# One set of sums instead of two: VectorE adds three tiles of probabilities into the buffer in which POOL adds the other five

## The chip, the core and the metric

The kernel runs on one core of a Trainium2 chip. The engines of the core work side by side and meet at semaphores: TensorE (PE in the profile; its weight loads are listed as PEld), VectorE (DVE), ScalarE (ACT), GpSimd (POOL) and SyncE (SP), which issues the DMAs. The metric is the device time of one execution in microseconds (us).

## The reference

A transformer block on x of 4 batches x 1024 tokens x 128 columns, all float32:

```
x = x + attention(layernorm(x))
x = x + ffn(layernorm(x))

attention: qkv = xn @ w_qkv; 16 heads of 64; q and k rotated (RoPE)
           scores = q k^T / 8;  probs = softmax(scores)     # over 1024 keys
           out = (probs @ v) @ w_out + b_out
ffn:       fp4_linear(silu(fp4_linear(x, w_gate)) * fp4_linear(x, w_up), w_down)
           # activations and weights rounded to FP4 in blocks of 16, then multiplied
```

The change concerns one quantity of the softmax: for each query and head, the sum of the exponentials over the 1024 keys.

## The kernel before

Attention takes most of the kernel. Its unit is a **pair**: two heads of one batch, so 4 x 8 = 32 pairs, P = 0 to 31. The 1024 queries of a pair are cut into two **halves** c = 0, 1 of 512, its keys into eight tiles jt = 0 to 7 of 128. One **exp step** i = 8c + jt (16 in a pair) is: eight score matmuls into PSUM `st` (keys on partitions, 512 queries, both heads), one exponential on ScalarE from `st` into one of eight slots of the ring `probs`, and the products with `v` into PSUM `po`. The scores carry the row maximum as a fourth product with `max_rows`, so that the exponential needs no further subtraction. Row maxima come from separate score matmuls, one pair ahead: TensorE fills `mx` (L1099), VectorE reduces it to `negmax` (L800). There is a single `mx`, so a fill waits until the reduction of the fill before is done (semaphore `mx_free`), 16 times in a pair.

All engines walk over the same two loops, written out by hand: over pairs, and in a pair over d = 0 to 7. On TensorE a d is: a fill of `mx`, the scores of two exp steps, a second fill of `mx`, one small unit of preparation or finishing through the PSUM bank `ms`, the products with v of the two steps before, and perhaps a second unit. The units are given by a table: K (d = 0 to 3, projection of keys and queries of pair P+2, then rotated on VectorE at L832 and L833), V (d = 4, 5), O (d = 6, 7, output projection of pair P-1, added on VectorE at L847), B (the maxima are transposed, L1106, and VectorE spreads them into `max_rows`, L814; at d = 2 for the second half of P, at d = 6 for the first half of P+1), and S (the softmax sums, L1115; at d = 5 for the first half of P, at d = 1 for the second half of P-1). In a few pairs X and Y units transpose the next batch's and the finished batch's rows.

The sum over keys of one half is made in three places. VectorE adds tiles 0 and 1 (`first_keys`, L822) into `first_sum`, one instruction for each of the two heads, at d = 1 and 3 for the first half and at d = 5 and 6 for the second. POOL adds tiles 2 and 3 into `psum_keys` and then tiles 4 to 7 to it, one at a time (`add_step`, L352), five instructions for each half; on POOL's queue they stand among the rotations (L483), the low parts of the heads (L487), the normalisation of the output (L478) and, in the pairs P = 13, 14, 21, 22, 29 and 30, three instructions that round FP4 values (`round_y`, L367 to L369), which stand between the add of tile 3 and that of tile 4. TensorE then sums over the partitions by products with ones (`softmax_sums`, L1115), four for `first_sum` and four for `psum_keys`, in one accumulation group. An exponential may overwrite a slot of the ring only when the product with v and the adder of that tile are done (L595 to L598).

The semaphore `key_part` counts VectorE's instructions, `key_sum` POOL's. After the last pair a second stage (the FFN) follows on the same engines, whose start on TensorE stands behind the last S unit.

Of the kernel before, what the change touches and what calls it, by code (L numbers as in the profile page):

```python
# [11 lines left out]
ALU = mybir.AluOpType  # L12
# [21 lines left out]
FIRST_KEYS = 2  # L34
# [22 lines left out]
def block_program(nc, ctx, x_d, gamma_d, beta_d, wqkv_d, wout_d, bout_d, wg_d, wu_d, wd_d,  # L57
# [34 lines left out]
    first_sum = sb("first_sum", [PART, 2, 2, CH])  # L92
# [35 lines left out]
    h_exp = [t[:, :].rearrange("p c a n -> p (c a n)")[:, 0:GT * FFN] for t in (psum_keys, first_sum)]  # L128
# [78 lines left out]
    def keys_added(P, c):  # L207

        return (JT - FIRST_KEYS - 1) * (2 * P + c)
# [119 lines left out]
    def _(pool):  # L329
# [10 lines left out]
        def add_step(P, i):  # L340
            c, jt = i // JT, i % JT
            if jt <= FIRST_KEYS:
                return
            wait(pool, exp_done, STEPS * P + i + 1)
            if jt == FIRST_KEYS + 1:
                if P > 0:
                    filled(pool, ("S", P - 1, c))
                first = probs[:, (STEPS * P + i - 1) % RING]
            else:
                pool.wait_ge(key_sum, keys_added(P, c) + jt - FIRST_KEYS - 1)  # L350
                first = psum_keys[:, c]
            nc.gpsimd.tensor_tensor(psum_keys[:, c], first, probs[:, (STEPS * P + i) % RING], ALU.add)\  # L352
              .then_inc(key_sum, 1)
# [187 lines left out]
    def _(act):  # L541
# [47 lines left out]
        def exp(P, i):  # L589
            step_n = STEPS * P + i  # L590
            act.wait_ge(st_ps, step_n + 1)
            if step_n >= RING:
# [4 lines left out]
                else:  # L597
                    act.wait_ge(key_sum, keys_added(old, c) + max(jt - FIRST_KEYS, 1))  # L598
# [92 lines left out]
    def _(dve):  # L691
# [126 lines left out]
        def first_keys(P, c, a):  # L818
# [3 lines left out]
            nc.vector.tensor_reduce(first_sum[:, c, a], probs[:, 0:FIRST_KEYS, a].rearrange("p r n -> p n r"), AX.X,  # L822
# [26 lines left out]
        def pair(P):  # L849
            F = P - 1  # L850
            for d in range(JT):
# [6 lines left out]
                for kind, X, u in units_at(P, d):  # L858
                    if kind == "K":
                        rope_parts(X, u)  # L860
                    if kind == "B":
                        spread_maxima(X, u)
                    if kind == "O" and present(P):
                        accumulate(X, u)
                if present(P) and d in (1, 3, 5, 6):
                    first_keys(P, d // HALF, int(d in (3, 6)))
# [136 lines left out]
    def _(pe):  # L1003
# [104 lines left out]
        def softmax_sums(F, c):  # L1108
            bank(("S", F, c))
            pe.wait_ge(key_part, 2 * (2 * F + c) + 2)  # L1110
            pe.wait_ge(key_sum, keys_added(F, c + 1))
            for part in (first_sum, psum_keys):
                for j in range(4):
                    a, quarter = j // 2, bass.ts(j % 2, QUARTER)
                    last = mm(ms[32 * j:32 * j + 32, 0:QUARTER], ones[:, 0:32], part[:, c, a, quarter],  # L1115
                              start=part is first_sum, stop=part is psum_keys)
# [153 lines left out]
```

## Time and profile before

| | |
|---|---|
| median of 3 runs | 1718.77 us (1718.58 to 1719.2) |
| profiled execution | 1719.78 us, its span 1718.0 us |
| granted TensorE clock, mean | 0.979 of full |
| PE busy | 93% of the span |
| POOL busy | 75% |
| DVE busy | 69% |
| ACT busy | 42% |

The profile is of one execution. Busy time is the time in which an engine had an instruction in work; matmuls are pipelined, so that two rows of TensorE overlap a little, and the distance between starts says more than a duration. A wait in brackets at the end of a row of a timeline is idle time of the engine just before the row, with what ended it.

### The profile page before, as it was taken

How to read it: one execution, taken by the hardware profiler on the slowest of the kernel's cores; microseconds unless marked ns; L12 is line 12 of the kernel's file. 1: busy time of each engine (PE TensorE's matmuls, PEld its weight loads, DVE VectorE, ACT ScalarE, POOL GpSimd, SP SyncE). 2: the span in 40 equal slices, each digit the busy share in tenths (PEclk: the TensorE clock that was granted, in tenths of full speed). 3: DMA queues.
4: the chain of work that ended last, by engine and by line, in shares of the span. 5: the costliest groups of instructions: out<-in, count | busy, mean ns of one | idle time of the engine just before them, and what ended most of it. 6: DMA issues, size and time to landing. Idle time of an engine off the chain costs nothing.

```text
span 1718.0 us, 26114 instructions
## 1 busy us (share of the span) xinstructions
PE 1605.0 (93%) x10025; PEld 863.4 (50%) x10025; DVE 1180.9 (69%) x1440; ACT 722.2 (42%) x941; POOL 1294.3 (75%) x729
## 2 busy tenths in 40 slices
PE   3899999999999999999999999999999999997666
PEld 1455555555555555555545555555555545554454
DVE  4877776666667677766667767766667777654676
ACT  1244444544444544544444445444444534443222
POOL 4478888777778878887777878797777788865674
PEclk9799999999999999999999999999999999998888
DMA  4111111111111111111111111111111111100000
GB/s 123 42 38 33 44 44 43 38 45 44 40 35 35 44 33 44 44 36 44 45 44 40 26 44 36 40 44 39 42 45 44 40 36 34 27 16 21 13 13 25
DMA packets 69194, 67.12 MB, mean 39 GB/s; under 512 B 26512, under 2 KB 52432, under 8 KB 69072
## 3 DMA queue, kind: packets, MB, share of 16 engines
q1 hardware_dynamic: 69072, 65.46, 15.2%
q8 instruction: 80, 1.31, 0.3%
q14 instruction: 42, 0.34, 0.1%
HBM read 29.25 MB, written 2.62 MB: 19 GB/s over the span
## 4 chain that ended last, share of the span: by engine, by line
PE 83%; DVE 13%; POOL 1%; issue 1%; ACT 1%; DMA 0%; DVEq 0%; POOLq 0%
PE po L1059 27%; PE st L1047 24%; PE mx L1099 9%; PE ms L1082 8%; PE ms L1070 4%; PE ms L1115 4%; PE ms L1124 4%; DVE negmax L800 3%; DVE first_sum L822 2%; DVE max_rows L814 1%; PE ms L1106 1%; PE mx L1183 1%; DVE probs L756 1%; PE st L1183 1%; DVE amax L750 1%
## 5 line engine op out<-in xcount | busy, mean ns | idle before, releaser
L800 DVE TENSOR_REDUCE negmax<-mx 128x2 f32<-128x1024 f32 x504 | 615.6, 1221 | 376.4 <-PE mx L1099 376.4
L599 ACT ACTIVATE probs<-st 128x1024 f32<-128x1024 f32 x512 | 497.8, 1023 | 533.6 <-PE st L1047 533.6
L352 POOL TENSOR_TENSOR psum_keys<-psum_keys,probs 128x1024 f32<-128x1024 f32 x256 | 607.4, 2373 | 127.4 <-ACT probs L599 109.3
L1059 PE MATMUL po<-probs,v 128*64 128x512 f32 x2048 | 495.7, 605 | 0.0
L1047 PE MATMUL st<-heads 64*128 64x512 f32 x3072 | 440.0, 391 | 0.0
L1047 PEld LDWEIGHTS st<-heads 64*128 64x128 f32 x3072 | 289.9, 185 | 58.4 <-issue 2.4
L1099 PE MATMUL mx<-heads 64*128 64x512 f32 x1008 | 230.1, 452 | 29.7 <-DVE negmax L800 29.5
L1059 PEld LDWEIGHTS po<-probs,v 128*64 128x64 f32 x2048 | 124.2, 136 | 256.2 <-issue 147.0
L352 POOL TENSOR_TENSOR psum_keys<-probs 128x1024 f32<-128x1024 f32 x64 | 151.7, 2370 | 87.1 <-ACT probs L599 87.0
L1047 PE MATMUL st<-max_rows,one_rows 64*128 64x512 f32 x1024 | 201.9, 389 | 0.0
L1099 PEld LDWEIGHTS mx<-heads 64*128 64x128 f32 x1008 | 94.8, 184 | 186.3 <-issue 117.3
L483 POOL TENSOR_TENSOR kq<-kq 128x1024 f32<-128x1024 f32 x64 | 152.3, 2379 | 40.8 <-DMA kq<-sin_part 40.7
L1082 PE MATMUL ms<-xnT,wqkv 128*128 128x512 f32 x256 | 150.9, 673 | 15.4 <-DVE sin_part L833 13.5
L822 DVE TENSOR_REDUCE first_sum<-probs 128x512 f32<-128x1024 f32 x128 | 159.4, 1245 | 5.1 <-ACT probs L599 5.1
L487 POOL TENSOR_TENSOR heads<-kq,heads 128x1024 fp32r<-128x1024 f32 x64 | 153.6, 2401 | 0.0
L478 POOL TENSOR_TENSOR oT<-oT,rsum 128x512 f32<-128x512 f32 x64 | 82.8, 1293 | 84.7 <-DMA rsum<-recips 83.2
L1047 PEld LDWEIGHTS st<-max_rows,one_rows 64*128 64x128 f32 x1024 | 96.9, 185 | 21.8
L832 DVE TENSOR_TENSOR kq<-ms,cos 128x512 f32<-128x512 f32 x128 | 87.4, 683 | 17.7 <-issue 9.0
L814 DVE TENSOR_TENSOR max_rows<-ms,mask 128x512 fp32r<-128x512 f32 x64 | 44.3, 691 | 70.7 <-PE ms L1106 70.7
L611 ACT ACTIVATE sums_kept<-ms 128x256 f32<-128x256 f32 x64 | 24.6, 385 | 151.4 <-PE ms L1115 151.4
L833 DVE TENSOR_TENSOR sin_part<-ms,sin 128x512 f32<-128x512 f32 x128 | 87.0, 680 | 0.0
L617 ACT ACTIVATE oT<-po 128x512 f32<-128x512 f32 x64 | 38.3, 599 | 109.8 <-PE po L1059 109.8
(144 smaller groups left out, 1237.0 us busy)
## 6 DMA issues: line engine op xcount, KB each, us to landing
kq<-sin_part SPq DMA_DIRECT2D x256, 128.0 KB, 2.4
rsum<-recips SPq DMA_DIRECT2D x128, 128.0 KB, 2.9
wqkv<-in_L_attn_w_qkv_dram SPq DMA_DIRECT2D x32, 192.0 KB, 2.8
resid<-in_L_attn_x_dram SPq DMA_DIRECT2D x4, 512.0 KB, 8.3
wout<-in_L_attn_w_out_dram SPq DMA_DIRECT2D x32, 64.0 KB, 2.6
out_dram<-resid SPq DMA_DIRECT2D x8, 256.0 KB, 2.3
sums<-sums_kept SPq DMA_DIRECT2D x64, 4.0 KB
spread<-sums SPq DMA_DIRECT2D x64, 4.0 KB, 1.5
```

Source lines behind the costliest of these rows:

```text
L352: nc.gpsimd.tensor_tensor(psum_keys[:, c], first, probs[:, (STEPS * P + i) % RING], ALU.add)\
L483: nc.gpsimd.tensor_tensor(raw[s], raw[s], swp[s], ALU.add).then_inc(rotated, 1)
L487: nc.gpsimd.tensor_tensor(heads[:, L % SETS, s, 1], raw[s], heads[:, L % SETS, s, 0].bitcast(F32), ALU.subtract)\
L599: nc.scalar.activation(probs[:, step_n % RING], st[step_n % 2][:, :], ACT.Exp, scale=SCALE)\
L800: nc.vector.tensor_reduce(negmax[:, t // HALF, :, t % HALF, half], banks[:, :], AX.X, ALU.max, negate=True)\
L822: nc.vector.tensor_reduce(first_sum[:, c, a], probs[:, 0:FIRST_KEYS, a].rearrange("p r n -> p n r"), AX.X, ALU.add).then_inc(key_part, 1)
L832: nc.vector.tensor_tensor(raw[s][:, part], ms[:, :], cos[:, part], ALU.mult).then_inc(cos_done, 1)
L833: nc.vector.tensor_tensor(sin_part[:, s, part], ms[:, :], sin[:, part], ALU.mult).then_inc(ms_free, 1)
L1047: last = mm(st[step_n % 2][:, a], stationary[rows], moving[rows], start=(n == 0), stop=(n == 3))
L1059: last = mm(po[HD * a:HD * a + HD, :], v[:, P % 2, jt, HD * a:HD * a + HD], probs[:, step_n % RING, a], start=(jt == 0), stop=(jt == JT - 1))
L1082: mm(ms[:, :], wqkv[:, L % 2, 1 - s, :], batch(L)[:, bass.ts(c, CH)], start=True, stop=True)\
L1099: last = mm(banks[:, a, :], heads[rows, N % SETS, 1, 0, bass.ts(t, PART)], heads[rows, N % SETS, 0, 0, bass.ts(half, CH)], start=True, sto ...
```

## The change

VectorE now adds three tiles, 0 to 2, and writes the sum into `psum_keys` itself. POOL adds the five tiles 3 to 7 to that, still five instructions for each half; the first of them now waits for both of VectorE's instructions of that half. TensorE multiplies one buffer with ones, four products for each half and not eight. VectorE's four instructions of a pair stand at d = 1, 2, 5 and 6 (before: 1, 3, 5 and 6), and at d = 2 and 6 in front of `spread_maxima`, where before `spread_maxima` stood in front of the one at d = 6. The old buffer stays as a work buffer of the FFN.

```diff
-FIRST_KEYS = 2
+FIRST_KEYS = 3
...
     def keys_added(P, c):
-        return (JT - FIRST_KEYS - 1) * (2 * P + c)
+        return (JT - FIRST_KEYS) * (2 * P + c)
...
         def add_step(P, i):
             c, jt = i // JT, i % JT
-            if jt <= FIRST_KEYS:
+            if jt < FIRST_KEYS:
                 return
             wait(pool, exp_done, STEPS * P + i + 1)
-            if jt == FIRST_KEYS + 1:
-                if P > 0:
-                    filled(pool, ("S", P - 1, c))
-                first = probs[:, (STEPS * P + i - 1) % RING]
-            else:
-                pool.wait_ge(key_sum, keys_added(P, c) + jt - FIRST_KEYS - 1)
-                first = psum_keys[:, c]
-            nc.gpsimd.tensor_tensor(psum_keys[:, c], first, probs[:, (STEPS * P + i) % RING], ALU.add)\
+            if jt == FIRST_KEYS:
+                pool.wait_ge(key_part, 2 * (2 * P + c) + 2)
+            wait(pool, key_sum, keys_added(P, c) + jt - FIRST_KEYS)
+            nc.gpsimd.tensor_tensor(psum_keys[:, c], psum_keys[:, c], probs[:, (STEPS * P + i) % RING], ALU.add)\
               .then_inc(key_sum, 1)
...
-                    act.wait_ge(key_sum, keys_added(old, c) + max(jt - FIRST_KEYS, 1))
+                    act.wait_ge(key_sum, keys_added(old, c) + jt - FIRST_KEYS + 1)
...
-            nc.vector.tensor_reduce(first_sum[:, c, a], probs[:, 0:FIRST_KEYS, a].rearrange("p r n -> p n r"), AX.X,
+            nc.vector.tensor_reduce(psum_keys[:, c, a], probs[:, 0:FIRST_KEYS, a].rearrange("p r n -> p n r"), AX.X,
                                     ALU.add).then_inc(key_part, 1)
...
                 for kind, X, u in units_at(P, d):
                     if kind == "K":
                         rope_parts(X, u)
+                    if kind == "O" and present(P):
+                        accumulate(X, u)
+                if present(P) and d in (1, 2, 5, 6):
+                    first_keys(P, d // HALF, int(d in (2, 6)))
+                for kind, X, u in units_at(P, d):
                     if kind == "B":
                         spread_maxima(X, u)
-                    if kind == "O" and present(P):
-                        accumulate(X, u)
-                if present(P) and d in (1, 3, 5, 6):
-                    first_keys(P, d // HALF, int(d in (3, 6)))
...
         def softmax_sums(F, c):
             bank(("S", F, c))
-            pe.wait_ge(key_part, 2 * (2 * F + c) + 2)
             pe.wait_ge(key_sum, keys_added(F, c + 1))
-            for part in (first_sum, psum_keys):
-                for j in range(4):
-                    a, quarter = j // 2, bass.ts(j % 2, QUARTER)
-                    last = mm(ms[32 * j:32 * j + 32, 0:QUARTER], ones[:, 0:32], part[:, c, a, quarter],
-                              start=part is first_sum, stop=part is psum_keys)
+            for j in range(4):
+                a, quarter = j // 2, bass.ts(j % 2, QUARTER)
+                last = mm(ms[32 * j:32 * j + 32, 0:QUARTER], ones[:, 0:32], psum_keys[:, c, a, quarter],
+                          start=True, stop=True)
             last.then_inc(ms_full, 1)
```

On VectorE at d = 2, between the two reductions of `mx`, the order before was this (L832 and L833 are the rotation, L814 the spreading of the maxima):

```order
L800 TENSOR_REDUCE negmax<-mx 128x2 [waits mx_full] x2
L832 TENSOR_TENSOR kq<-ms,cos 128x512 [waits swap_q_in,lo_done,ms_full]
L833 TENSOR_TENSOR sin_part<-ms,sin 128x512
L814 TENSOR_TENSOR max_rows<-ms,mask 128x512 [waits st_ps,ms_full]
L800 TENSOR_REDUCE negmax<-mx 128x2 [waits mx_full] x2
```

The same place after (four lines are gone above, so L796, L828, L829, L818 and L810 are the old L800, L832, L833, L822 and L814):

```order
L796 TENSOR_REDUCE negmax<-mx 128x2 [waits mx_full] x2
L828 TENSOR_TENSOR kq<-ms,cos 128x512 [waits swap_q_in,lo_done,ms_full]
L829 TENSOR_TENSOR sin_part<-ms,sin 128x512
L818 TENSOR_REDUCE psum_keys<-probs 128x512 [waits exp_done]
L810 TENSOR_TENSOR max_rows<-ms,mask 128x512 [waits st_ps,ms_full]
L796 TENSOR_REDUCE negmax<-mx 128x2 [waits mx_full] x2
```

A sum of keys has come in, in front of the spreading.

On VectorE at d = 6 it was (L847 adds the output projection):

```order
L800 TENSOR_REDUCE negmax<-mx 128x2 [waits mx_full] x2
L847 TENSOR_TENSOR resid<-ms,resid 128x512 [waits ms_free,ms_full]
L814 TENSOR_TENSOR max_rows<-ms,mask 128x512 [waits st_ps,ms_full]
L822 TENSOR_REDUCE first_sum<-probs 128x512 [waits exp_done]
L800 TENSOR_REDUCE negmax<-mx 128x2 [waits mx_full] x2
```

And after:

```order
L796 TENSOR_REDUCE negmax<-mx 128x2 [waits mx_full] x2
L843 TENSOR_TENSOR resid<-ms,resid 128x512 [waits ms_free,ms_full]
L818 TENSOR_REDUCE psum_keys<-probs 128x512 [waits exp_done]
L810 TENSOR_TENSOR max_rows<-ms,mask 128x512 [waits st_ps,ms_full]
L796 TENSOR_REDUCE negmax<-mx 128x2 [waits mx_full] x2
```

The sum of keys and the spreading have changed places.

On POOL the adds of a pair's first half were, with the rotation L483 among them:

```order
L352 TENSOR_TENSOR psum_keys<-probs 128x1024 [waits ms_full,exp_done]
L352 TENSOR_TENSOR psum_keys<-psum_keys,probs 128x1024 [waits key_sum,exp_done] x3
L483 TENSOR_TENSOR kq<-kq 128x1024 [waits swap_k_in,cos_done]
L352 TENSOR_TENSOR psum_keys<-psum_keys,probs 128x1024 [waits key_sum,exp_done]
L478 TENSOR_TENSOR oT<-oT,rsum 128x512 [waits po_copied,recips_in]
```

And are now:

```order
L348 TENSOR_TENSOR psum_keys<-psum_keys,probs 128x1024 [waits key_sum,key_part,exp_done]
L348 TENSOR_TENSOR psum_keys<-psum_keys,probs 128x1024 [waits key_sum,exp_done] x3
L479 TENSOR_TENSOR kq<-kq 128x1024 [waits swap_k_in,cos_done]
L348 TENSOR_TENSOR psum_keys<-psum_keys,probs 128x1024 [waits key_sum,exp_done]
L474 TENSOR_TENSOR oT<-oT,rsum 128x512 [waits po_copied,recips_in]
```

Nothing has moved in the queue; the first add waits for `key_part`.

## Rows read from the trace of the kernel before

**Rows 1.** The page, busy time by engine: us (share of the span) xinstructions.

```profile
PE 1605.0 (93%) x10025; PEld 863.4 (50%) x10025; DVE 1180.9 (69%) x1440; ACT 722.2 (42%) x941; POOL 1294.3 (75%) x729
```

**Rows 2.** Waits over the whole span: total us, times, longest.

```profile
PE mx L1099 <- DVE negmax L800: 29.5, 35, 3.5
```

**Rows 3.** Timeline of PE, P = 14, d = 1 to 5, and d = 1 after: start, us, ...

```profile
735.92 0.64 PE L1115 MATMUL ms<-first_sum,ones 128*32 128x256 f32 x8
736.38 0.61 PE L1115 MATMUL ms<-psum_keys,ones 128*32 128x256 f32 x8
736.92 0.50 PE L1099 MATMUL mx<-heads 64*128 64x512 f32 x2
...
739.09 0.40 PE L1099 MATMUL mx<-heads 64*128 64x512 f32 x2
739.42 1.13 PE L1082 MATMUL ms<-xnT,wqkv 128*128 128x512 f32 x2
...
744.79 0.39 PE L1099 MATMUL mx<-heads 64*128 64x512 f32 x2
...
758.98 0.64 PE L1115 MATMUL ms<-first_sum,ones 128*32 128x256 f32 x8
...
783.66 0.64 PE L1115 MATMUL ms<-first_sum,ones 128*32 128x256 f32 x8
```

**Rows 4.** Timeline of DVE, P = 14, d = 1 and 2.

```profile
735.69 1.24 DVE L822 TENSOR_REDUCE first_sum<-probs 128x512 f32<-128x1024 f32 x1
737.47 1.23 DVE L800 TENSOR_REDUCE negmax<-mx 128x2 f32<-128x1024 f32 x1 [0.54 <-PE mx L1099]
...
741.27 0.68 DVE L833 TENSOR_TENSOR sin_part<-ms,sin 128x512 f32<-128x512 f32 x1
742.71 0.69 DVE L814 TENSOR_TENSOR max_rows<-ms,mask 128x512 fp32r<-128x512 f32 x1 [0.75 <-PE ms L1106]
```

**Rows 5.** Timeline of DVE, P = 14, d = 6.

```profile
763.74 0.68 DVE L847 TENSOR_TENSOR resid<-ms,resid 128x512 f32<-128x512 f32 x1
765.81 0.69 DVE L814 TENSOR_TENSOR max_rows<-ms,mask 128x512 fp32r<-128x512 f32 x1 [1.39 <-PE ms L1106]
766.42 1.26 DVE L822 TENSOR_REDUCE first_sum<-probs 128x512 f32<-128x1024 f32 x1
767.60 1.22 DVE L800 TENSOR_REDUCE negmax<-mx 128x2 f32<-128x1024 f32 x1
```

**Rows 6.** Timeline of PE, P = 14, d = 7.

```profile
765.70 0.50 PE L1099 MATMUL mx<-heads 64*128 64x512 f32 x2
...
768.86 0.50 PE L1099 MATMUL mx<-heads 64*128 64x512 f32 x2 [0.80 <-DVE negmax L800]
769.29 1.16 PE L1124 MATMUL ms<-wout,oT 128*128 128x128 f32 x8
```

**Rows 7.** Groups by line and shape, DVE: busy us, mean ns.

```profile
L750 DVE TENSOR_REDUCE amax<-probs 128x88 f32<-128x1408 f32 x8 | 12.9, 1614 | 0.1
```

**Rows 8.** Timeline of DVE, P = 1, d = 1.

```profile
120.57 0.86 DVE L712 BATCH_NORM_STATS2 ln_columns<-resid 128x6 f32<-128x128 f32 x4
```

**Rows 9.** Timeline of POOL, P = 14, d = 1 to 4.

```profile
736.30 1.29 POOL L367 TENSOR_TENSOR xnT<-xnT,y_exp 128x512 f32<-128x512 f32 x1
...
740.06 4.91 POOL L352 TENSOR_TENSOR psum_keys<-psum_keys,probs 128x1024 f32<-128x1024 f32 x2
...
747.49 2.38 POOL L483 TENSOR_TENSOR kq<-kq 128x1024 f32<-128x1024 f32 x1
749.82 2.37 POOL L352 TENSOR_TENSOR psum_keys<-psum_keys,probs 128x1024 f32<-128x1024 f32 x1
```

**Rows 10.** Timeline of DVE, last pair, d = 6.

```profile
1558.19 1.23 DVE L822 TENSOR_REDUCE first_sum<-probs 128x512 f32<-128x1024 f32 x1
```

**Rows 11.** Timeline of POOL, last pair, tiles 4 to 7 of the second half.

```profile
1556.69 9.90 POOL L352 TENSOR_TENSOR psum_keys<-psum_keys,probs 128x1024 f32<-128x1024 f32 x4 [1.64 <-ACT probs L599]
```

**Rows 12.** Timeline of PE, last S unit.

```profile
1566.74 0.64 PE L1115 MATMUL ms<-first_sum,ones 128*32 128x256 f32 x8 [0.61 <-POOL psum_keys L352]
```

More of the change, by code:

```diff
@@ L91, in block_program @@
     probs = sb("probs", [PART, RING, 2, CH])
-    first_sum = sb("first_sum", [PART, 2, 2, CH])
+    tail_work = sb("tail_work", [PART, 2, 2, CH])
     psum_keys = sb("psum_keys", [PART, 2, 2, CH])
@@ L127, in block_program @@
     hT = probs_flat[:, 4 * GT * FFN:4 * GT * FFN + GT * 3 * PART]
-    h_exp = [t[:, :].rearrange("p c a n -> p (c a n)")[:, 0:GT * FFN] for t in (psum_keys, first_sum)]
+    h_exp = [t[:, :].rearrange("p c a n -> p (c a n)")[:, 0:GT * FFN] for t in (psum_keys, tail_work)]
     st = [ctx.enter_context(nc.psum_tensor(f"st{i}", [PART, 2, CH], F32)) for i in range(2)]
```

## The prediction

> **What bounds the kernel now.** I read the page's busy shares first: PE is busy 93% of the span [rows 1], so what TensorE does not issue is time won, and what it waits for is time lost. Second, the list of waits: in attention TensorE waits for little else than VectorE's reductions of `mx`, 35 times, 29.5 us [rows 2]. Third, the timelines of PE, DVE and POOL over one pair, P = 14, since the list doesn't say at which d. The reader is to see there that in each pair TensorE is held once: the second fill of `mx` at d = 7 starts 3.16 us after the first [rows 6], where at d = 2 it is 2.17 [rows 3]. I counted 31 such waits of 0.79 to 0.82 us, one in each pair but the last. Their cause is VectorE at d = 6: it idles 1.39 us for the transposed maxima, spreads them, and only then sums keys, so that the reduction of `mx` comes late [rows 5]. POOL has slack; its adds set no time before the last pair, where the last S unit waits 0.61 us for them [rows 12].
>
> **The products with ones.** An S unit is two groups, the second 0.46 us behind the first, the next fill of `mx` 0.54 behind the second [rows 3]. One group goes. If the one that stays keeps the longer distance, 0.46 is won, otherwise up to 0.54. I take 0.46, for 64 units: **-29.4** (to -34.6).
>
> **The price of a third tile on VectorE.** It appears in no row. A reduction of 1408 elements takes 1.61 us [rows 7], one of 1024 takes 1.23 with two outputs and 1.24 to 1.26 with 512 [rows 4, 5]: it goes by what is read, 1.0 ns an element. 1536 elements give 1.24 + 0.53 = 1.77. The next instruction starts 0.08 before a row's end (766.42 + 1.26 against 767.60), so the sum holds the queue 1.69 to 1.70 us, where it held 1.16 to 1.18. From below the bound is 1.24 (price by outputs), from above 1.5 x 1.245 = 1.87 (nothing fixed); the row with 1408 is nearest, I take 1.77.
>
> The Trainium skill (VectorE: DVE Perf Modes, "The TRN2 errata") gives 58 cycles and one per element at 0.96 GHz for an instruction that reads SBUF, 1.66 us for 1536 elements. By the same formula 1024 elements would take 1.13, and the row shows 1.24, so the row decides. With 1.66 the sum below would be some 10 us better, 1698.
>
> **VectorE at d = 1 and 2.** How a late reduction hurts is in rows 6: it ends at 768.82, the fill starts 0.04 later, and the next unit 0.43 after the fill, where it is 0.33 otherwise [rows 3]. So a wait costs its lateness plus 0.10. At d = 1 the sum starts at 735.69 as now, the next reduction at 737.39 instead of 737.47 [rows 4], but TensorE comes 0.46 earlier. The reduction ends at 738.61, the second fill is possible at 738.65 and due at 739.09 - 0.46 = 738.63 [rows 3]: 0.12 lost, 30 pairs, **+3.6**. In P = 0 and 1 four statistics stand behind the sum, 0.78 on the queue [rows 8]: **+1.6**.
> At d = 2 a whole sum is new. In the clock of the trace before, the last product of the rotation frees the queue at 741.87, the sum runs to 743.57, covering the 0.75 of idle time [rows 4]; spreading 0.61, reduction 1.22, fill at 745.44, due at 744.79 [rows 3]: 0.65 + 0.10 = 0.75 for each of the 30 pairs with K units, and 0.6 in P = 30: **+23.1**. That it left d = 3 gives nothing: there VectorE was in time. After d = 3 it has caught up.
>
> **VectorE at d = 6.** The sum now starts behind the addition, 763.74 + 0.61 = 764.35, and lies in the idle 1.39 us [rows 5]. It ends at 766.05, spreading at 766.66, reduction 767.88, fill 767.92, due at 765.70 + 2.17 = 767.87. Lost 0.05 + 0.10 = 0.15 instead of 0.99 + 0.10 = 1.09 [rows 6]: 0.94 won in 31 pairs, **-29.1**.
>
> **POOL.** Its first add waited for an exponential of d = 1 and now waits for the sum at d = 2, about 743.65 + 0.12 + 0.1 = 743.9, some 9 us later; behind it in the queue stand the other adds, the rotations, the low parts and the normalisation. Four adds of 2.5 (4.91 for two, one 2.37 [rows 9]), rotation 2.33, add 2.37: tile 7 done at 758.6. The S unit of d = 5 is due at 758.98 + 0.12 + 0.75 = 759.85 [rows 3]: 1.3 us of cover, no cost. The second half in the same way: VectorE's sum 766.6 (0.12 + 0.75 - 0.46 later than above), an add and a low part 4.7, four adds 9.9, done 781.2, due at 783.66 + 0.41 - 0.94 = 783.1 [rows 3]; this pair has a Y unit of 0.6, the others 1.3 us of cover. Who waits for what stands behind the adds (the rotated and low parts, the ring slots) wants it later than the S units want the sum.
> The cover is gone in two places. Where `round_y` stands between the adds, POOL needs 3.76 more [rows 9] and is at 762.2: 2.35 us of waiting in five pairs, 1.1 in P = 30: **+12.9**; the scaling of `y` in three pairs costs about **+0.3**. And in the last pair nothing is left behind which POOL could hide: VectorE's sum waits there for the addition of d = 6 and starts at 1558.19 [rows 10]. POOL's first add of that half, which ran before 1556.69 [rows 11], starts at 1558.19 + 1.77 + 0.1 = 1560.1, five take 12.4, S at 1572.6 instead of 1566.74 [rows 12], and the FFN behind it, where VectorE is the first to have work: **+5.9**.
>
> **Sum.** -29.4 - 29.1 + 3.6 + 1.6 + 23.1 + 12.9 + 0.3 + 5.9 = -11.1. From the profiled 1719.78 that is 1708.7; the median of the runs shown lies 1.0 below that execution, so 1707.7.
>
> **Rivals.**
> - *The third tile costs half of the first two* (1.87 us). Each 0.1 us more on this sum costs at d = 1, 2 and 6, about 91 times: +9, so 1717. For it: no row has this shape with three. Against: 1408 elements in 1.61.
> - *The third tile is free*, 1.24 us, as far as 512 outputs set the price. d = 1 costs nothing, d = 2 0.22 for 30 pairs, d = 6 wins its whole 1.09: 1681. Against it stand rows 7.
> - *POOL is late at every S unit* (slower). The place is the start of tile 3's add; cover is 1.3 us, and 57 S units have only that. If the hand-over from VectorE and the five adds take 1.7 us more than worked out, 57 x 0.5 + 6 x 1.7 = 39 are added: 1746. It decides from 1.5 us on. For it: a chain of 15 us on POOL now starts at a fixed point with no idle time in it. Against: all adds take 2.37 us or 2.5 behind one another, whatever VectorE does beside them [rows 9, 11].
> - *The rounding and the last pair cost less than worked out*, because something in these pairs moves with POOL: without the 12.9, 1695.
>
> **How the numbers follow.** The forecast has 0.72, the costly third tile 0.10, the free one 0.04, POOL late at every S unit 0.08, no cost in the rounding pairs 0.06. The range of 8 in 10 goes from 1695 (longer saving on the products, no cost in the rounding pairs) to 1719 (the costly tile with the small waits doubled). About 0.2% (3.4 us) is what a measurement can tell from no change: faster than 1715.3 holds for most of the forecast, the free tile and the last rival, 0.79; the costly tile and a small part of the forecast fall within, 0.12; slower 0.09.
>
> **What would show it.** In the changed profile: L1111 with 4 x 64 products of weights, 8 matmul rows an S unit and the next fill 0.54 behind its start; L818 at 1.77 us; the wait of 0.80 at d = 7 gone, and one of about 0.5 idle at d = 3 in its place; POOL's first add released by DVE; S units that wait over 2 us for POOL only near the six rounding pairs; the last S unit held some 6 us. A sum of keys at 1.9 or more, or a wait for POOL at ordinary S units, would make the forecast wrong.

## The result, and the profile after

| | before | changed |
|---|---|---|
| median | 1719.39 us (10 runs, 1716.95 to 1720.7) | 1722.95 us (10 runs, 1721.7 to 1725.57) |
| span of the profiled execution | 1718.0 us | 1720.2 us |
| ratio to before, 95% interval | | 1.0023 (1.0013 to 1.0032) |

The change made the kernel slower by 3.6 us, where 11 us less was forecast: wrong sign, and outside the range. The forecast of 1707.7 is out by 15 us.

Busy time by engine on the page of the changed kernel, as in [rows 1]:

```profile
PE 1589.5 (92%) x9513; PEld 846.0 (49%) x9513; DVE 1256.0 (73%) x1440; ACT 722.8 (42%) x941; POOL 1293.1 (75%) x729
```

TensorE has its 512 fewer matmul rows. VectorE is busy 75 us more in all. Its 128 sums alone take 244.4 us; at the 1.24 to 1.26 of [rows 4, 5] they took 160, so each is 0.66 longer, where I had 0.53 (the sums grew by 85 us; 10 are taken back by more overlap of rows and by slightly shorter other rows). The group of these sums on the page (busy us, mean ns, idle before):

```profile
L818 DVE TENSOR_REDUCE psum_keys<-probs 128x512 f32<-128x1536 f32 x128 | 244.4, 1910 | 9.2 <-ACT probs L595 9.2
```

**1.91 us, not 1.77**, and more than the upper bound of 1.87. This row is where the forecast failed. The waits of TensorE in the changed kernel (total, times, longest), to be read beside [rows 2]:

```profile
PE mx L1096 <- DVE negmax L796: 23.3, 33, 3.5
PE ms L1110 <- POOL psum_keys L348: 18.1, 11, 6.6
```

The first total is hardly lower than before, but the waits are other ones. The timeline of PE in P = 14, d = 1 to d = 7, answers to [rows 3, 6]:

```profile
729.98 0.64 PE L1110 MATMUL ms<-psum_keys,ones 128*32 128x256 f32 x8
730.55 0.49 PE L1096 MATMUL mx<-heads 64*128 64x512 f32 x2
...
732.84 0.50 PE L1096 MATMUL mx<-heads 64*128 64x512 f32 x2
...
739.41 0.49 PE L1096 MATMUL mx<-heads 64*128 64x512 f32 x2 [0.61 <-DVE negmax L796]
...
755.99 1.08 PE L1110 MATMUL ms<-psum_keys,ones 128*32 128x256 f32 x8 [2.26 <-POOL psum_keys L348]
757.00 0.79 PE L1096 MATMUL mx<-heads 64*128 64x512 f32 x2
...
763.83 0.51 PE L1096 MATMUL mx<-heads 64*128 64x512 f32 x2
...
766.16 0.49 PE L1096 MATMUL mx<-heads 64*128 64x512 f32 x2
```

The S unit takes 0.57 us to the next fill instead of 1.00. At d = 7 the two fills are 2.33 apart, no longer 3.16: the old wait is gone. In its place the second fill of d = 3 (739.41) waits 0.61, and in this rounding pair the S unit waits 2.26 for POOL. The timeline of DVE at d = 2 and at d = 6 shows the cause, beside [rows 4, 5]:

```profile
735.72 1.91 DVE L818 TENSOR_REDUCE psum_keys<-probs 128x512 f32<-128x1536 f32 x1
737.54 0.69 DVE L810 TENSOR_TENSOR max_rows<-ms,mask 128x512 fp32r<-128x512 f32 x1
738.14 1.22 DVE L796 TENSOR_REDUCE negmax<-mx 128x2 f32<-128x1024 f32 x1
...
762.47 1.90 DVE L818 TENSOR_REDUCE psum_keys<-probs 128x512 f32<-128x1536 f32 x1
764.29 0.68 DVE L810 TENSOR_TENSOR max_rows<-ms,mask 128x512 fp32r<-128x512 f32 x1
764.89 1.21 DVE L796 TENSOR_REDUCE negmax<-mx 128x2 f32<-128x1024 f32 x1
```

A sum holds the queue 1.82 us, from its start to that of the spreading.

**An ordinary pair, by four marks.** The transposition B and the S unit each stand once in each half of a pair, so their starts cut it into four pieces. Before, PE:

```profile
860.29 0.33 PE L1106 MATMUL ms<-ident,maxcol 128*128 128x128 f32 x1
877.92 0.64 PE L1115 MATMUL ms<-first_sum,ones 128*32 128x256 f32 x8
...
884.34 0.33 PE L1106 MATMUL ms<-ident,maxcol 128*128 128x128 f32 x1
900.93 0.64 PE L1115 MATMUL ms<-first_sum,ones 128*32 128x256 f32 x8
...
907.41 0.33 PE L1106 MATMUL ms<-ident,maxcol 128*128 128x128 f32 x1
```

The same pair in the changed kernel:

```profile
857.24 0.33 PE L1103 MATMUL ms<-ident,maxcol 128*128 128x128 f32 x1
874.06 0.64 PE L1110 MATMUL ms<-psum_keys,ones 128*32 128x256 f32 x8
880.28 0.33 PE L1103 MATMUL ms<-ident,maxcol 128*128 128x128 f32 x1
897.76 0.64 PE L1110 MATMUL ms<-psum_keys,ones 128*32 128x256 f32 x8
903.78 0.33 PE L1103 MATMUL ms<-ident,maxcol 128*128 128x128 f32 x1
```

The pieces went from 17.63, 6.42, 16.59 and 6.48 us to 16.82, 6.22, 17.48 and 6.02. The first holds the wait of d = 7 (-0.81, -0.84 in most pairs), the second an S unit and the new lateness at d = 2 (-0.20), the third the wait of d = 3 (+0.89), the fourth an S unit alone (-0.46, -0.44 in most). A pair is 0.58 shorter; the forecast was 0.99 (0.92 and 0.94 won, 0.12 and 0.75 lost).

### The profile page after: what moved, and what is told of

Its sections match the earlier page's. It is cut to its first block, busy times and chain, and to the rows that moved or that the text cites. A ratio compares the mean times of both kernels' runs of the same rounds, so it can differ in the third digit from the quotient of the medians.

```text
span 1720.2 us, 25092 instructions
## 1 busy us (share of the span) xinstructions
PE 1589.5 (92%) x9513; PEld 846.0 (49%) x9513; DVE 1256.0 (73%) x1440; ACT 722.8 (42%) x941; POOL 1293.1 (75%) x729
## 4 chain that ended last, share of the span: by engine, by line
PE 65%; DVE 14%; POOL 11%; issue 7%; ACT 1%; DMA 1%; SPq 1%; POOLq 0%; DVEq 0%; ACTq 0%
PE st L1044 21%; PE po L1056 19%; PE mx L1096 8%; POOL psum_keys L348 8%; PE ms L1079 5%; PE ms L1119 3%; PE ms L1067 3%; DVE psum_keys L818 3%; DVE negmax L796 3%; PE ms L1110 2%; DVE kq L828 1%; DVE sin_part L829 1%; PE mx L1178 1%; DVE max_rows L810 1%; DVE probs L752 1%
## 5 line engine op out<-in xcount | busy, mean ns | idle before, releaser
L348 POOL TENSOR_TENSOR psum_keys<-psum_keys,probs 128x1024 f32<-128x1024 f32 x320 | 762.3, 2382 | 311.4 <-issue 241.6
L796 DVE TENSOR_REDUCE negmax<-mx 128x2 f32<-128x1024 f32 x504 | 616.6, 1223 | 366.9 <-PE mx L1096 366.9
L595 ACT ACTIVATE probs<-st 128x1024 f32<-128x1024 f32 x512 | 497.8, 1024 | 536.1 <-PE st L1044 536.1
L1096 PE MATMUL mx<-heads 64*128 64x512 f32 x1008 | 235.9, 464 | 23.3 <-DVE negmax L796 23.3
L818 DVE TENSOR_REDUCE psum_keys<-probs 128x512 f32<-128x1536 f32 x128 | 244.4, 1910 | 9.2 <-ACT probs L595 9.2
L483 POOL TENSOR_TENSOR heads<-kq,heads 128x1024 fp32r<-128x1024 f32 x64 | 151.6, 2369 | 0.0
L828 DVE TENSOR_TENSOR kq<-ms,cos 128x512 f32<-128x512 f32 x128 | 87.5, 683 | 17.7 <-issue 9.0
L829 DVE TENSOR_TENSOR sin_part<-ms,sin 128x512 f32<-128x512 f32 x128 | 87.0, 680 | 0.0
L618 ACT ACTIVATE heads<-kq 128x1024 fp32r<-128x1024 f32 x64 | 67.3, 1052 | 28.9 <-POOL kq L479 28.9
L1067 PE MATMUL ms<-wqkv,xnT 128*128 128x128 f32 x512 | 74.1, 288 | 1.7 <-DVE sin_part L829 1.7
```

The source lines that it names most:

```text
L348: nc.gpsimd.tensor_tensor(psum_keys[:, c], psum_keys[:, c], probs[:, (STEPS * P + i) % RING], ALU.add)\
L483: nc.gpsimd.tensor_tensor(heads[:, L % SETS, s, 1], raw[s], heads[:, L % SETS, s, 0].bitcast(F32), ALU.subtract)\
L595: nc.scalar.activation(probs[:, step_n % RING], st[step_n % 2][:, :], ACT.Exp, scale=SCALE)\
L796: nc.vector.tensor_reduce(negmax[:, t // HALF, :, t % HALF, half], banks[:, :], AX.X, ALU.max, negate=True)\
L818: nc.vector.tensor_reduce(psum_keys[:, c, a], probs[:, 0:FIRST_KEYS, a].rearrange("p r n -> p n r"), AX.X, ALU.add).then_inc(key_part, 1)
L828: nc.vector.tensor_tensor(raw[s][:, part], ms[:, :], cos[:, part], ALU.mult).then_inc(cos_done, 1)
```

## The experiments

**What three tiles cost.** `r_shapes`, one run; behind VectorE's last instruction of the kernel before:

```diff
+        for r in (2, 3, 4, 5):
+            total(scratch[r - 2], probs[:, 0:r, 0].rearrange("p r n -> p n r"))
+        for r in (2, 3, 4):
+            total(scratch[r + 2], probs_flat[:, 0:r * CH].rearrange("p (n r) -> p n r", r=r))
+        total(scratch[7][:, 0:256], probs_flat[:, 0:1536].rearrange("p (n r) -> p n r", r=6))
+        total(scratch[7][:, 256:258], probs_flat[:, 0:1536].rearrange("p (n r) -> p n r", r=768))
+        link(nc.vector.tensor_tensor(scratch[0], probs[:, 0, 0], probs[:, 1, 0], ALU.add))
+        link(nc.vector.tensor_tensor(scratch[0], scratch[0], probs[:, 2, 0], ALU.add))
```

> The kernel before, with nine reductions and two additions on VectorE behind its last instruction, the other engines idle; only their durations are looked at. The trace after shows 1.91 us for the sum of three tiles, 1.24 for two. Theory A (the price is set per output, and three addends of one output cost more than three reads): strided 512x2 1.24, 512x3 1.91, contiguous 512x3 also 1.91, while the same 1536 elements as 256x6 or 2x768 take about 1.75; 512x4 about 2.3 and 512x5 about 2.9, close to the line of the reads. Theory B (the distance of 4 KB between the tiles costs): strided 512x3 1.91, contiguous 512x3 1.75, and 512x2 contiguous below 1.24. Theory C (VectorE was disturbed by POOL's adds in the kernel): here all of 1536 elements take 1.75, the strided one too. The two additions of 512 elements should take 0.69 each.

Its groups by shape, DVE (busy us, mean ns). Those into `first_sum` are the sums over strided tiles, those into `psum_keys` have their addends side by side:

```profile
L1004 DVE TENSOR_REDUCE first_sum<-probs 128x512 f32<-128x2560 f32 x1 | 4.5, 4471 | 0.0
L1004 DVE TENSOR_REDUCE first_sum<-probs 128x512 f32<-128x2048 f32 x1 | 3.6, 3619 | 0.0
L1004 DVE TENSOR_REDUCE psum_keys<-probs 128x512 f32<-128x2048 f32 x1 | 2.3, 2286 | 0.0
L1004 DVE TENSOR_REDUCE first_sum<-probs 128x512 f32<-128x1536 f32 x1 | 1.9, 1912 | 0.0
L1004 DVE TENSOR_REDUCE psum_keys<-probs 128x512 f32<-128x1536 f32 x1 | 1.8, 1753 | 0.0
L1004 DVE TENSOR_REDUCE psum_keys<-probs 128x256 f32<-128x1536 f32 x1 | 1.8, 1753 | 0.0
L1004 DVE TENSOR_REDUCE psum_keys<-probs 128x2 f32<-128x1536 f32 x1 | 1.8, 1753 | 0.0
L1004 DVE TENSOR_REDUCE first_sum<-probs 128x512 f32<-128x1024 f32 x1 | 1.2, 1232 | 0.0
L1012 DVE TENSOR_TENSOR first_sum<-probs 128x512 f32<-128x512 f32 x1 | 0.7, 691 | 0.0
```

Theory B holds as far as addends that lie apart cost more than addends side by side; A and C fall. None of them foresaw 3.619 us for four tiles. With addends side by side 1536 elements take 1.753 us with 512, 256 or 2 outputs, close to what I had worked out; with the addends apart 1.912, on an otherwise idle core. The extra is small for three (9%) and large for four (58%), so it isn't a line that could be drawn from the row with two.

`r_strides`, one run, asked whether the distance matters:

```diff
+        for r, strides in ((3, (512, 528, 768, 1024, 1040, 1088, 1536, 2048)), (4, (512, 528, 1024, 1040, 1536, 2048))):
+            for s in strides:
+                view = probs_flat[:, 0:r * s].rearrange("p (r s) -> p s r", s=s)[:, 0:CH, :]
```

> The kernel before, with fourteen sums of 512 outputs behind VectorE's last instruction, three or four addends each, at distances of 512, 528, 768, 1024, 1040, 1088, 1536 and 2048 elements between addends. Known so far: three at 1024 elements 1.912 us, three side by side 1.753, four at 1024 3.619 against 2.286 side by side, two 1.232 against 1.220. Theory B1 (addends whose distance is a multiple of some power of two of bytes meet in one place of the buffer and are read in turns): 512, 1024, 1536 and 2048 cost the extra, 528, 1040 and 1088 go at 1.753 and 2.286. Theory B2 (any distance costs, since the reads aren't side by side): all of three at about 1.91, all of four at about 3.62.

```profile
L1006 DVE TENSOR_REDUCE first_sum<-probs 128x512 f32<-128x2048 f32 x4 | 14.5, 3615 | 0.1
L1006 DVE TENSOR_REDUCE psum_keys<-probs 128x512 f32<-128x1536 f32 x4 | 7.6, 1912 | 0.1
L1006 DVE TENSOR_REDUCE first_sum<-probs 128x512 f32<-128x1536 f32 x4 | 7.6, 1912 | 0.1
```

All eight distances took 1.91 with three addends, all six 3.6 with four (B2): padding the ring would not help. Why addends apart cost more isn't settled.

**One part at a time.** `s_half`: the kernel before, without the four products of `first_sum`.

```diff
-            for part in (first_sum, psum_keys):
+            for part in (psum_keys,):
```

> The kernel before, with the four products of first_sum left out of each S unit (the sums lack tiles 0 and 1), nothing moved. My theory: TensorE's saving is real and whole, 0.44 us for each of 64 units as the trace after shows between its S units and the next transposition, less at the last unit: 28 us less than before, about 1691, and the waits of 0.80 at d = 7 stay. Rival (the saving is given back, because VectorE or POOL then come later in relation to TensorE): d = 2 or d = 7 shows longer waits for the reduction of mx, and less than 20 us is won.

1692.74 us, ratio 0.9844 (0.9827 to 0.986): 26.6 less than before. The saving is real, 0.42 for each unit, and the waits for `mx` stay (29.8 us in total, 29.5 before).

`order_d6`: the kernel before, with only the order at d = 6 changed.

```diff
-                    if kind == "B":
-                        spread_maxima(X, u)
                     if kind == "O" and present(P):
                         accumulate(X, u)
                 if present(P) and d in (1, 3, 5, 6):
                     first_keys(P, d // HALF, int(d in (3, 6)))
+                for kind, X, u in units_at(P, d):
+                    if kind == "B":
+                        spread_maxima(X, u)
```

> The kernel before, with only the order at d = 6 changed: VectorE sums its two tiles in front of the spreading of the maxima; two tiles, two buffers and the places d = 1, 3, 5, 6 stay. My theory: the wait of 0.80 at d = 7 goes whole, 1.09 us in 31 pairs, 33 us less: about 1686. Rival (something else holds the second fill at d = 7 when VectorE is in time, or VectorE is late for the transposed maxima): less than 20 us is won, with a wait left at d = 7 in the list.

1682.15 us, ratio 0.9783 (0.9769 to 0.9798): **37 less than before**. Between its marks the piece that holds d = 7 is 1.05 to 1.15 shorter in nearly all pairs, as worked out (1.09). These pieces make up 34.9 of the 37.5 us by which the profiled span is shorter; 1.8 more lie behind the last S unit and are not explained. DVE at d = 6:

```profile
748.19 1.23 DVE L822 TENSOR_REDUCE first_sum<-probs 128x512 f32<-128x1024 f32 x1
749.66 0.69 DVE L814 TENSOR_TENSOR max_rows<-ms,mask 128x512 fp32r<-128x512 f32 x1 [0.24 <-PE ms L1107]
```

A sum of two tiles fits into the idle time and leaves 0.24 of it; one of three, 0.66 longer, does not.

`two_tiles`: the changed kernel, with a sum that reads two tiles (tile 2 is missing from the sums).

```diff
-            nc.vector.tensor_reduce(psum_keys[:, c, a], probs[:, 0:FIRST_KEYS, a].rearrange("p r n -> p n r"), AX.X,
+            nc.vector.tensor_reduce(psum_keys[:, c, a], probs[:, 0:2, a].rearrange("p r n -> p n r"), AX.X,
```

> The changed kernel, with the sum of VectorE reading two tiles and not three (tile 2 is left out of the sums); all waits, the order and the number of products as changed. It takes the price of the third tile away, 0.67 us on each of 128 sums. My theory: at d = 2 the loss of 0.24 goes, at d = 3 it falls from 0.87 to 0.20, at d = 7 the rest of 0.25 goes: 1.15 less in 30 pairs, 35 us less than the changed kernel, about 1688; waits for POOL at the S units of the rounding pairs and the last pair stay. Rival (the time goes to POOL's late start, not to VectorE's own length): less than 12 us is won.

1686.14 us, ratio to before 0.9812 (0.9796 to 0.9827), 36.8 less than the changed kernel. Between the marks an ordinary pair loses 0.66 at d = 3, 0.23 at d = 7 and 0.22 at d = 2, where 0.67, 0.25 and 0.24 were expected. So the third tile itself costs 37 us. That is over half of what TensorE and the new order win; POOL's late start, below, takes most of the rest.

**All three tiles, in less time.** `tt_sum`: the changed kernel, with two additions in place of the reduction.

```diff
-            nc.vector.tensor_reduce(psum_keys[:, c, a], probs[:, 0:FIRST_KEYS, a].rearrange("p r n -> p n r"), AX.X,
-                                    ALU.add).then_inc(key_part, 1)
+            link(nc.vector.tensor_tensor(psum_keys[:, c, a], probs[:, 0, a], probs[:, 1, a], ALU.add))
+            nc.vector.tensor_tensor(psum_keys[:, c, a], psum_keys[:, c, a], probs[:, 2, a], ALU.add)\
+              .then_inc(key_part, 1)
```

> The changed kernel, with VectorE's sum of three tiles made by two additions of 512 elements and not by one reduction. Alone such an addition took 0.69 us, the reduction 1.91. My theory: it is VectorE's length at d = 1, 2 and 6 that made the change lose; the queue is held about 1.3 us and not 1.82, so most of what reading two tiles gave (37 us) comes back with all three tiles in the sum: 30 to 37 us less than the changed kernel, about 1689. Rival: the additions read two operands from the same memory as POOL's adds and keep each other out, up to one POOL instruction of 2.37 us each time; then they take 1 to 3 us at d = 1 and 5, where POOL is busy, and the kernel is slower than the changed one, over 1725. The Trainium skill (SBUF — State Buffer, "Who interferes with whom") states that rival for a VectorE instruction with two SBUF inputs and a POOL instruction that reads SBUF; no run so far shows it.

1748.73 us, ratio 1.0164 (1.015 to 1.0178): my theory fell here, and the rival holds. Its DVE at d = 2 and d = 5:

```profile
751.17 0.68 DVE L818 TENSOR_TENSOR psum_keys<-probs 128x512 f32<-128x512 f32 x1
751.89 0.69 DVE L819 TENSOR_TENSOR psum_keys<-psum_keys,probs 128x512 f32<-128x512 f32 x1
...
767.13 1.93 DVE L818 TENSOR_TENSOR psum_keys<-probs 128x512 f32<-128x512 f32 x1
769.09 2.72 DVE L819 TENSOR_TENSOR psum_keys<-psum_keys,probs 128x512 f32<-128x512 f32 x1
```

And its POOL at the same time as the second two:

```profile
768.46 2.79 POOL L348 TENSOR_TENSOR psum_keys<-psum_keys,probs 128x1024 f32<-128x1024 f32 x1
771.22 1.72 POOL L474 TENSOR_TENSOR oT<-oT,rsum 128x512 f32<-128x512 f32 x1
```

Where POOL idles (d = 2, 6) an addition takes 0.68 to 0.69 in nearly all pairs. Where POOL is at work (d = 1, 5) both engines take longer: VectorE's second addition 1.65 us at the median and the longest of all 2.92, POOL 2.79 for 2.37 and 1.72 for 1.29. The Trainium skill (SBUF — State Buffer, "Who interferes with whom") states such an exclusion for VectorE with two SBUF inputs against a POOL instruction that reads SBUF, and none for `tensor_reduce`; by that rule, the trace agrees: these additions grow from 0.69 to 1.65 and more, while all 128 reductions of the changed kernel took 1.90 to 1.93.

`tt_where_idle`: the additions only for `a == 1`, at d = 2 and 6.

```diff
+            if a == 1:
+                link(nc.vector.tensor_tensor(psum_keys[:, c, a], probs[:, 0, a], probs[:, 1, a], ALU.add))
+                nc.vector.tensor_tensor(psum_keys[:, c, a], psum_keys[:, c, a], probs[:, 2, a], ALU.add)\
+                  .then_inc(key_part, 1)
+                return
```

> The changed kernel, with the two additions only for the second head's sum, at d = 2 and d = 6, where POOL idles and waits for this very sum; at d = 1 and 5 the reduction stays. In the run with additions everywhere those at d = 2 and 6 took 0.69 us each, those at d = 1 and 5 up to 2.8. My theory: the queue is held 1.33 us and not 1.82, so the loss at d = 3 falls from 0.87 to 0.38 and the rest of 0.25 at d = 7 goes; some 0.7 us in 31 pairs, 22 us less than the changed kernel, about 1701. Rival (POOL's adds and VectorE's additions meet here too as soon as VectorE is quicker): additions of over 1 us at d = 2 and 6, and under 8 us won.

1702.21 us, ratio 0.9898 (0.9882 to 0.9915): 20.7 less than the changed kernel, 1 from the forecast. Its additions:

```profile
L819 DVE TENSOR_TENSOR psum_keys<-probs 128x512 f32<-128x512 f32 x64 | 45.2, 707 | 0.0
L820 DVE TENSOR_TENSOR psum_keys<-psum_keys,probs 128x512 f32<-128x512 f32 x64 | 44.3, 692 | 2.2
```

0.49 us less on the queue at two places of a pair gave 21 us: the account by length holds with all the data in the sum.

**POOL's late start.** `round_late` moved the rounding behind POOL's add of tile 7, `last_first` moved VectorE's last sum of pair 31 in front of the addition, `both` did both, `round_early` moved the rounding in front of the add of tile 3.

```diff
-            if (P % PPB, i) in ((5, 4), (6, 4)):     # changed kernel
+            if (P % PPB, i) in ((5, 9), (6, 9)):     # round_late, both
+            if (P % PPB, i) in ((5, 2), (6, 2)):     # round_early, best
                 round_y(2 * b + P % PPB - 5)
...
                     if kind == "O" and present(P):
+                        if P == PAIRS - 1 and d == 6:     # last_first, both, best
+                            first_keys(P, 1, 1)
                         accumulate(X, u)
```

> The changed kernel, with POOL's three rounding instructions moved from between the adds of tiles 3 and 4 to behind the add of tile 7 (i = 9), where POOL waits for VectorE anyway. My theory: it takes away the waits of S for POOL in the six rounding pairs, 1.2, 2.3, 1.2, 2.3, 2.3 and 1.2 us in the trace after, and in the one or two of them behind which the granted clock fell to 0.60 some 1.5 us more: 10.5 to 14 us less than the changed kernel, about 1709 to 1713. Rival (POOL's late start is felt elsewhere as soon as these waits go, at the low parts or at the transposition of y at d = 7): under 5 us.

1739.23 us, ratio 1.0114 (1.01 to 1.0128), 16 more than the changed kernel: a new wait of my own making. DVE in P = 13, d = 4:

```profile
707.95 1.40 DVE L755 TENSOR_SCALAR y_exp<-xnT 128x512 int32<-128x512 int32 x1 [8.95 <-POOL xnT L365]
```

VectorE waits there for the rounding before it may prepare the next group, and the reductions of `mx` stand behind it. TensorE's waits for them grew from 23.3 to 45.4 us, while the S units' waits for POOL fell from 18.1 to 7.8.

> The changed kernel, with VectorE's last sum of keys (pair 31, d = 6) put in front of the addition of the output projection, for which it waits 7 us there. My theory: POOL's last five adds start 4 to 5 us earlier, the last S unit waits 2 us and not 6.56, and the clock does not fall behind it: 4.5 to 6.5 us less than the changed kernel, about 1717. Rival (the FFN's start is set by VectorE or by the reciprocals, not by the last S unit): under 2 us.

1718.43 us, ratio 0.9995 (0.9986 to 1.0003), 4.5 less than the changed kernel; the last S unit waits 2.45 and not 6.56. The clock still fell (0.68 granted in the 4.3 us behind it), against my expectation; in `both`, next, the same unit waits 2.43 and 1.00 is granted behind it.

> The changed kernel with both edits, the later rounding and the earlier last sum. If the two losses are apart, as I hold, they add up: 15 to 20 us less than the changed kernel, about 1705, and no wait for POOL over 1 us is left in the list but the last. If they are one (the same clock falls, or one late POOL), less than the sum.

1734.81 us, ratio 1.0087 (1.0073 to 1.0101). The two add up (16.3 lost, 4.5 won, 11.9 measured), but the first has the other sign.

> The changed kernel, with POOL's rounding in front of the add of tile 3 (i = 2), where POOL idles 5.9 us for VectorE's sum. The later place (i = 9) cost 16 us, since VectorE's preparation of the next group at d = 4 waits for the rounding. My theory: this place has both: the waits of S for POOL in the rounding pairs go, 10.4 us, and the fall of the clock behind one or two of them: 10 to 14 us less than the changed kernel, about 1711. Rival (normalisation or the low parts behind the rounding are then late): under 5 us.

1709.95 us, ratio 0.9936 (0.9924 to 0.9949): 13 less than the changed kernel. The S units that wait for POOL fell from 11 to 3.

> The changed kernel with three edits: the sum by two additions, the rounding at i = 2, the last pair's last sum in front of the addition. If my terms are right they add: 33 + 12 + 4.5 less than 1723, about 1673, below the 1682.2 of the order at d = 6 alone. If the additions and POOL keep each other out it is above 1700.

1730.0 us, ratio 1.0049 (1.0036 to 1.0063). It had the additions everywhere, and they spoilt it; against `tt_sum` the two other edits won 18.7, about as alone (13.0 + 4.5).

**What is left of the scheme.** `mixed`: the first half as before, the second as changed, with the order of `order_d6` and the last sum first.

```diff
-FIRST_KEYS = 2
+FIRST_KEYS = (2, 3)
...
-                if present(P) and d in (1, 3, 5, 6):
+                if present(P) and d in (1, 3, 5, 6) and (P, d) != (PAIRS - 1, 6):
...
-            for part in (first_sum, psum_keys):
+            for part in (first_sum, psum_keys)[c:]:
```

> A version made from what the runs showed: the first half of each pair as in the kernel before (two tiles, two buffers, d = 1 and 3), the second half as changed (three tiles into psum_keys at d = 5 and 6, one product group), the sum of keys in front of the spreading at d = 6, and the last pair's last sum in front of the addition. Against the kernel with the order of d = 6 alone (1682.2) it wins 0.44 us at 31 S units, 13.6 us, and loses 0.25 at d = 7 of 31 pairs, 7.7, since the sum of three tiles is 0.67 longer and its cover there ends: about 1677. Rival (POOL's late start in the second half comes late to the S unit at d = 1): waits for POOL at ordinary S units, and slower than 1682.

1684.74 us, ratio 0.9796 (0.9782 to 0.9809), no better than `order_d6`. Between the marks each pair is 0.19 shorter (0.44 won, 0.25 lost), as expected, but three pairs are 1.1 longer and the last ones 2: POOL's roots of the variance come later, since its second half now ends later, and ScalarE and its exponentials wait for them. First `order_d6`, then `mixed`:

```profile
ACT xnT L577 <- POOL ln_columns L433: 2.8, 1, 2.8
...
ACT xnT L580 <- POOL ln_columns L436: 14.5, 4, 3.9
```

The changed kernel has this wait too (14.4 us, 4 times). There it hides behind the late reductions: in these three pairs `two_tiles` wins 0.27 at d = 3 and not 0.66.

`mixed_tt`: two additions for its sum at d = 6, and the roots at i = 0.

```diff
+            if c == 1 and a == 1:
+                link(nc.vector.tensor_tensor(psum_keys[:, c, a], probs[:, 0, a], probs[:, 1, a], ALU.add))
...
-            if (P % PPB, i) == (3, 1):
+            if (P % PPB, i) == (3, 0):
                 newton(ln_rstd[:, batch_rows(b)], batch_rows(b), b + 3)
```

> The version with the first half as before and the second half as changed (1684.7), with two edits: two additions for its sum at d = 6, and POOL's roots of the variance before the low parts (i = 0 and not 1) in the three pairs where ScalarE waited 3.9 us for them. My theory: 0.25 us at d = 7 in 31 pairs goes, 7.7 us, and part of 1.1 us in three pairs, 2: about 1675, 7 us below the 1682.2 of the order at d = 6 alone. Rival (POOL and VectorE meet at d = 6, or the low parts behind the roots come late): 1682 or more.

**1674.73 us, ratio 0.9739 (0.9725 to 0.9754)**, 44 less than the kernel before and the fastest of all. Between the marks against `mixed`, the additions won 7.4 us at d = 7 and the earlier roots 3.2 in the three pairs. The same wait in it:

```profile
ACT xnT L580 <- POOL ln_columns L436: 6.6, 4, 2.8
```

## Why the prediction was wrong

Term by term, from the trace of the changed kernel against that of before (span +2.2 us):

| step | forecast | measured | from |
|---|---|---|---|
| products with ones | -29.4 | -28 | 0.44 at 63 S units |
| d = 7 | -29.1 | -26 | 0.84 x 31 |
| d = 2 | +3.6 | +7 | 0.24 x 30 |
| d = 3 | +23.1 | +27 | 0.87 x 30, and P = 30 |
| P = 0 and 1 | +1.6 | +1.6 | |
| rounding, scaling of y | +13.2 | +11.4 | waits of 1.2, 2.3, 1.2, 2.3, 2.3, 1.2; 1.0 |
| last pair | +5.9 | +5.5 | |
| clock behind waits | 0 | +4.4 | 1.55 twice; 1.3 behind the last S unit, put down to the clock |
| three pairs with less waiting | 0 | -1.3 | |
| sum | -11.1 | +1.6 | |

0.6 us of the span is not in the table; the trace has a wait of 0.54 for POOL at the S unit of d = 1 in P = 30, which the table leaves out. The medians differ by 3.6, 1.4 more than the profiled spans. The ten executions of the changed kernel have mean granted clocks of 0.972 to 0.979, and the two longest (1725.57 and 1725.1 us) have the two lowest, 0.972 and 0.973; so part of the 1.4 may be the clock, which no run here separates.

- **The step that failed is "The price of a third tile on VectorE".** I drew it from a reduction of another shape [rows 7] and from sums of two addends [rows 5], and took the rest as proportional: 1.77, with a ceiling of 1.87. The addends lie apart, and three of them take 1.91. The sensitivity was worked out rightly: 0.14 us at d = 1, 2 and 6, 91 times, is 12.7, and the three rows of the table miss by 10.4. It was also the rival that I gave 0.10, at too low a price; with 1.91 in its place the sum is +1.6, and the forecast would have been no change. That the measured terms add up to the same +1.6 is chance: the three rows fall 2.3 short of 12.7, and the clock's +4.4 less the other rows' smaller misses happens to be 2.3. The mechanism was right and `two_tiles`, `tt_where_idle` and `r_shapes` show its size.
- **The clock was missing from the sum.** Behind some of the new waits TensorE's granted clock falls. Four stretches of the changed kernel just behind such waits: the length of the stretch, then PE, PEld, DVE, ACT and POOL busy, the granted clock, DMA share, GB/s:

```profile
755.99:760.30 4.31, 4.31 (x28) 2.82 (x28) 1.23 (x1) 1.14 (x2) 3.40 (x2) 0.60 0.02 2
1136.01:1140.30 4.29, 4.29 (x38) 3.06 (x40) 2.34 (x2) 2.32 (x3) 3.44 (x2) 1.00 0.02 2
1464.94:1469.20 4.26, 4.26 (x28) 2.98 (x28) 1.23 (x1) 1.41 (x2) 3.43 (x2) 0.62 0.02 2
1567.65:1572.00 4.35, 4.34 (x14) 2.25 (x15) 0.00 (x0) 0.85 (x2) 1.08 (x1) 0.52 0.02 2
```

  A wait of 2.26 us was followed by 0.60 and 0.62 twice (partly at 1.2 GHz, partly at 2.4) and by the full 2.4 GHz once; the last wait of 6.56 by 0.52. In P = 14 the piece from the S unit to B took 7.58 us, in an ordinary pair 6.02: 1.56 lost on top of the wait, and 1.55 in P = 29; in `round_early`, without the two waits, both are gone. I had priced the waits at their length, and the clock at nothing without a reason. That the 1.3 at the end is the clock's is not shown: in `round_early` the last wait is also 6.56 and the clock behind it 0.50, but the time from the last S unit to the end is 0.8 shorter. Nor does the length of such a wait tell whether the clock falls. In the changed kernel and `last_first` it fell in P = 14 and 29, in `two_tiles` in P = 14 and 22, in `tt_where_idle` in P = 22 and 29, each time behind waits of 2.25 to 2.28; behind the waits of 1.1 to 1.2 in these four it never did.
- **Right, and shown by runs of their own:** the saving on TensorE (`s_half`, 26.6 for 29.4), the wait of d = 7 as an effect of the order alone (`order_d6`, 1.09 a pair at the median for 1.09), POOL's late start, which ordinary S units do not feel and the rounding pairs and the last pair do (`round_early`, `last_first`). I had overlooked that two of the rounding pairs, P = 13 and 21, have X units at d = 3 and 4, which give POOL 1.2 us more; so they lost 1.2 where 2.35 was forecast.
- **The rivals:** that POOL is late at every S unit fell, ordinary S units don't wait; so did the free third tile, and that the rounding and the last pair cost less (11.4 and 5.5 measured). The argument against the first, that POOL's adds take the same "whatever VectorE does beside them", holds beside reductions only: in `tt_sum` they grew.
- **Slips in the working, none of which decides:** the lower bound of 1695 holds with one of its two reasons, both together give 1689.6. In the rounding pairs 758.6 + 3.76 is 762.4 and not 762.2, so the wait is 2.5 by its own terms (2.26 measured). The two rows of 1024 elements that were to show that the number of outputs doesn't matter differ in more than that, since `mx` lies in PSUM and `probs` in SBUF; `r_shapes` shows it within SBUF. The S unit of the changed kernel is L1110, not L1111.

What lost the time, then: the change bundled a good order (worth 37 us alone) and a smaller TensorE load (27 alone) with a longer sum on an engine whose queue at d = 1, 2 and 6 stands between TensorE and its next fill, at 0.67 us a sum 37 us, and with a later start for POOL, 17 us (`round_early` and `last_first` together).

These four leave 10 us won, where 3.6 were lost. The move of a sum from d = 3 to d = 2 has a price of its own, which no run tests alone: with two tiles (`two_tiles`) the piece that holds d = 3 is still 0.2 longer than in `order_d6` in ordinary pairs, an estimated 6 us in 30. What the two runs on POOL leave of its waits is about 3 more: the last S unit still waits 2.45 us, 1.8 more than before, and the scaling pairs keep their 1.0. The remaining 4 or so are not explained; they lie mostly behind the last S unit, where `order_d6` is 1.8 shorter than the kernel before and the changed kernel 1.3 longer.

## What to carry to other kernels

Price a longer instruction by its own access pattern, with addends as far apart as in the kernel, before it goes on a queue where every tenth of a microsecond counts ninety times. Ask of a change that moves and enlarges work at once what each part does alone: here the order alone won 37 us, and all the rest together lost it again. Before work is moved to where another engine idles, look at who waits for that engine's other results in the few irregular rounds; these, not the ordinary ones, paid for POOL's late start.

## What the runs showed of the hardware

- A VectorE reduction of float32 costs 1.04 ns for each further element with addends side by side (1.753 us for 1536, 2.286 for 2048), and the 1536 took the same with 2, 256 or 512 outputs. With addends apart, 512 outputs of 2, 3, 4 and 5 took 1.232, 1.912, 3.619 and 4.471 us, and those of 3 and 4 the same at any distance from 2 to 8 KB.
- An addition of two SBUF tiles of 512 float32 took 0.69 us, less than the reduction of the same two (1.23), but up to 2.9 where POOL was at work (`tt_sum`), whose instructions there took 2.79 for 2.37 and 1.72 for 1.29. In the changed kernel the reductions of three tiles kept to 1.90 to 1.93, beside POOL's instructions too.
- TensorE's granted clock, mean of the 4.3 us behind a wait of an S unit, was 0.60 to 0.65 in two of the three rounding pairs with a wait of 2.25 to 2.28 us, in each of four kernels, not always the same two, and 1.00 in the third; 1.00 behind waits of 1.1 to 1.2; 0.50 to 0.52 behind waits of 5.9 to 6.6.
